# A mixture of experts computed on chosen tokens only, in sorted blocks of 128

## The reference

```
h = _ln(x, ln_g, ln_b)
logits = h @ rw.T + rb
vals, idx = jax.lax.top_k(logits, K)          # K = 2 of E = 8
gates = jax.nn.softmax(vals, axis=-1)
h1 = jax.nn.gelu(jnp.einsum('nd,efd->enf', hf, fc1_w) + fc1_b[:, None, :], approximate=False)
eo = jnp.einsum('enf,edf->end', h1, fc2_w) + fc2_b[:, None, :]
gathered = eo[idx_f, jnp.arange(N)[:, None], :]
mixed = (gathered * gates_f[..., None]).sum(axis=1).reshape(x.shape)
return x + mixed
```

## Time and profile before

| | |
|---|---|
| three runs | 3813.97, 3814.2, 3821.2 us; median 3814.2 |
| profiled execution | 3820.08 us; span from first to last instruction 3818.3 us |
| TensorE busy | 3622.8 us (95%), 32576 instructions |
| VectorE busy | 2628.9 us (69%) |
| ScalarE busy | 2835.2 us (74%) |
| GpSimd busy | 990.7 us (26%) |
| granted TensorE clock | 0.989 of full speed, mean |

### The profile page before, as it was taken

How to read it: one execution, slowest core, us unless ns; L and a number is a source line. 1 busy time by engine, 2 the same in 40 slices (tenths; PEclk the granted TensorE clock), 3 DMA queues, 4 the chain that set the end, 5 groups by cost and what they waited for, 6 DMA issues and landing times.

```text
span 3818.3 us, 86916 instructions
## 1 busy us (share of the span) xinstructions
PE 3622.8 (95%) x32576; PEld 2540.8 (67%) x32576; DVE 2628.9 (69%) x5516; ACT 2835.2 (74%) x4951; POOL 990.7 (26%) x1348
## 2 busy tenths in 40 slices
PE   6889999999999999999999999999999999999987
PEld 3556677676666767676676676766766676667764
DVE  7775666767676776767767667676767767666644
ACT  4677778777877778778787877778778777877645
POOL 2221222223132132322213222231322313222222
PEclk9999999999999999999999999999999999999988
DMA  2001001000010010000100010010100100000100
GB/s 66 2 3 47 34 14 32 25 24 23 12 43 14 24 33 24 21 14 24 34 24 21 14 32 25 24 34 6 39 14 24 34 23 21 14 26 25 37 12 7
DMA packets 52615, 92.56 MB, mean 24 GB/s; under 512 B 11816, under 2 KB 35312, under 8 KB 51952
## 3 DMA queue, kind: packets, MB, share of 16 engines
q1 hardware_dynamic: 52208, 87.01, 7.0%
HBM read 82.80 MB, written 4.19 MB: 23 GB/s over the span
## 4 chain that ended last, share of the span: by engine, by line
PE 73%; DVE 11%; ACT 7%; POOL 3%; issue 3%; DMA 1%; SPq 1%; DVEq 0%; ACTq 0%; POOLq 0%
PE ps L1277 14%; PE ps L1354 10%; PE ps L1346 9%; PE ps L1289 8%; PE ps L1267 7%; PE ps L1297 3%; PE ps L1236 3%; DVE mx L1649 3%; PE ps L1262 3%; PE ps L1309 2%; ACT pt L1502 2%; DVE pr L1655 2%; PE ps L1245 2%; PE ps L1314 1%; ACT xh L1452 1%
## 5 line engine op out<-in xcount | busy, mean ns | idle before, releaser
L1649 DVE TENSOR_REDUCE mx<-ps 128x8 f32<-128x616 f32 (+1 forms) x704 | 671.6, 954 | 352.3 <-PE ps L1267 335.4
L1502 ACT ACTIVATE pt<-ps 77x512 f32<-77x512 f32 (+1 forms) x1408 | 764.8, 593 | 126.3 <-PE ps L1277 124.3
L1277 PE MATMUL ps<-k_sb,pr 128*77 128x128 f32 (+1 forms) x3776 | 532.0, 280 | 13.5 <-DVE qT L1628 4.4
L1840 POOL TENSOR_TENSOR kx<-kT,in_tiles 128x308 f32<-128x308 f32 (+1 forms) x384 | 313.5, 817 | 808.9 <-PE ps L1267 741.1
L1493 ACT ACTIVATE pr<-pr 128x616 f32<-128x616 f32 (+1 forms) x472 | 393.3, 841 | 149.7 <-DVE pr L1655 149.0
L1346 PE MATMUL ps<-hT,ew 128*128 128x512 f32 x1024 | 488.0, 600 | 7.2 <-ACT kx L1541 2.3
L1277 PEld LDWEIGHTS ps<-k_sb,pr 128*77 128x77 f32 (+1 forms) x3776 | 416.5, 146 | 117.5 <-issue 71.2
L1655 DVE TENSOR_TENSOR pr<-ps,mx 128x616 f32<-128x616 f32 (+1 forms) x472 | 450.3, 954 | 16.2
L1289 PE MATMUL ps<-pt,v 77*16 77x128 f32 (+2 forms) x11264 | 428.5, 276 | 18.4 <-ACT pt L1502 16.2
L1289 PEld LDWEIGHTS ps<-pt,v 77*16 77x16 f32 (+2 forms) x11264 | 255.0, 97 | 218.0 <-issue 118.2
L1511 ACT ACTIVATE og<-ps 128x256 f32<-128x256 f32 x704 | 261.7, 378 | 184.6 <-PE ps L1289 181.7
(11 more groups left out here) (174 smaller groups left out, 6004.2 us busy)
## 6 DMA issues: line engine op xcount, KB each, us to landing
ew<-weights SPq DMA_DIRECT2D x128, 512.0 KB, 4.7
x<-x SPq DMA_DIRECT2D x16, 256.0 KB, 3.1
out<-xh SPq DMA_DIRECT2D x16, 256.0 KB, 2.5
...
w_sb<-weights SPq DMA_DIRECT2D x1, 1542.0 KB, 10.8
...
```

The costliest lines, as they stand in the source:

```text
L1277: i = tr(p[0:keys, j * L:(j + 1) * L], probs[s][pl.slot(unit, 3)][:, c:c + keys], ident)
L1502: go_act(pt[s][0:keys, q % 2, :], p[0:keys, :], ACT.Copy).then_inc(probsT_ready.sem, 1)
L1649: link(v_.tensor_reduce(m, tile, AX.X, ALU.max, negate=True))
L1840: tell(pool, g_.tensor_tensor(spread_keys[s][:, pl.slot(step, 2), 0:4 * keys].rearrange("p (h k) -> p h k", h=4), kT[s][:, b * keys:(b + 1 ...
```

## The change

The experts are computed only on the (token, expert) pairs that were chosen: 1024 pairs per pass, sorted by expert, each expert's pairs padded to blocks of 128. `BLOCKS` = 15 blocks always suffice. For each pass:

- `pick` (VectorE) ranks the logits and marks the two chosen experts. `place` (eight narrow matmuls on TensorE, some 22 short operations on VectorE) counts them and gives each pair its row in the sorted order, and each block its expert.
- `scatter`: GpSimd issues eight indirect DMAs that write the normalized rows `xh` to `sorted_x` in HBM, 128 rows of 512 bytes each. `sorted`: SyncE loads all 15 blocks back (983 KB) when they have landed. `sort_turn`: TensorE turns them, ScalarE applies gain and bias.
- `fetch`: GpSimd issues an indirect DMA per block that fetches one expert's packed row of 1156 floats per partition (fc1, fc2, and both biases) into one of four slots of `ew`, 15 per pass. Slot j is free after block j - 4.
- `up` is four matmuls of 128 columns per block, then one bias sum on VectorE over 128x512 and one gelu on ScalarE. `down` is four matmuls, then one sum on VectorE with the second bias.
- `put`: SyncE writes the results to `sorted_y` in HBM in four DMAs. `get`: GpSimd issues eight indirect DMAs that fetch each token's two rows. `combine`: eight scaled sums on VectorE.
- Once at the start, SyncE's queue copies the experts into a packed table `experts` in HBM (four DMAs after the load of pass 3), and fills `sorted_x` of each stream with finite numbers (983 KB each), that of stream 0 ahead of the first weights.
- `gates`, `expert_bias` and the resident second bias `b2_sb` are gone. The planner's costs of several other steps are changed by a few hundredths, and its priority tables (`EAGER`, `CHANGES`, `STRETCH` 60 to 80) are others, so the order on all engines is another.

```diff
+BLOCKS = 2 * NB * L // 128 + NE - 1
+GROUPS = -(-BLOCKS // 4)
+SLOTS = 4
...
-    out += [("fetch", s, 0), ("fetch", s, 1)]
-    out += norm_steps(6, s) + [("route", s), ("gates", s), ("expert_bias", s)]
-    for e in range(0, NE, 2):
-        out += [("up", s, f, c) for f in (e, e + 1) for c in range(FC)]
-        out += [("down", s, e), ("down", s, e + 1)]
-        if e + 4 < NE:
-            out.append(("fetch", s, e // 2 + 2))
+    out += norm_steps(6, s) + [("route", s), ("pick", s), ("place", s), ("scatter", s)]
+    out += [("fetch", s, j) for j in range(SLOTS)] + [("sorted", s)] + [("sort_turn", s, c) for c in range(GROUPS)]
+    for j in range(BLOCKS + 1):
+        if j < BLOCKS:
+            out.append(("up", s, j))
+        if j:
+            out.append(("down", s, j - 1))
+            if j + SLOTS - 1 < BLOCKS:
+                out.append(("fetch", s, j + SLOTS - 1))
+            if j % 4 == 0 or j == BLOCKS:
+                out.append(("put", s, (j - 1) // 4))
+    out += [("get", s), ("combine", s)]
...
     if kind == "fetch":
+        return [(G, INDIRECT), (Y, 3.4)]
+    if kind in ("scatter", "get"):
+        return [(G, 2 * NB * INDIRECT), (Y, 2.2)]
+    if kind == "sorted":
         return [(Y, 5.0)]
+    if kind == "put":
+        return [(Y, 3.0)]
...
+        "pick": [(V, 1.9)], "place": [(P, 0.9), (V, 5.0)], "combine": [(V, 2.5)],
+        "sort_turn": [(P, 0.47), (A, act(n, 1.2))],
+        "up": [(P, pe(128, 4) + 0.02), (V, 0.72), (A, act(n))], "down": [(P, pe(D, 4) + 0.04), (V, 0.3)],
...
-STRETCH = 60
+STRETCH = 80
...
+            sp.dma_start(sorted_x[0].rearrange("(p j) d -> p (j d)", p=128), weights[:, 0:BLOCKS * D]).then_inc(cleared[0], 16)
...
+                elif kind == "sorted":
+                    sp.wait_ge(scattered[s], 16 * 2 * NB * (s // S + 1))
+                    sp.dma_start(blocks[s], sorted_x[s].rearrange("(j p) d -> p j d", p=128)).then_inc(sorted_in[s], 16)
+                elif kind == "put":
+                    lo, hi = 4 * step[2], min(4 * step[2] + 4, BLOCKS)
+                    sp.wait_ge(*down_ready(s, hi - 1))
+                    sp.dma_start(sorted_y[s][lo * 128:hi * 128].rearrange("(j p) d -> p j d", p=128), blocks[s][:, lo:hi, :])\
+                        .then_inc(returned[s], 16)
...
+                    if s == S - 1:
+
+                        by_expert = experts.rearrange("(e p) n -> p e n", p=128)
+                        for name, source in (("fc1", weights[:, W_FC1:W_FC1 + NE * FF]), ("fc2", weights[:, W_FC2:W_FC2 + NE * FF]),
+                                             ("fc1_b", cols[:, C_AT["L1_fc1_b"][0]:C_AT["L1_fc1_b"][0] + NE * FC])):
+                            o, n = E_AT[name]
+                            sp.dma_start(by_expert[:, :, o:o + n], source.rearrange("p (e n) -> p e n", e=NE)).then_inc(packed, 16)
...
+                elif kind == "place":
+                    (s,) = args
+                    pe.wait_ge(*picked(s))
+                    flat = chosen[s][:].rearrange("p b e -> p (b e)")
+                    n = NB * NE
+                    mm(p[:, 0:n], K("upto"), flat, start=True, stop=False)
+                    for d in range(1, NB):
+                        mm(p[:, d * NE:n], ones[:], flat[:, 0:n - d * NE], start=False, stop=d == NB - 1)
                     for b in range(NB):
-                        i = tr(p[0:NE, b * L:(b + 1) * L], gates[s][:, b, :], ident)
-                    i.then_inc(gates_turned.sem, 1)
-                elif kind == "expert_bias":
-                    (s,) = args
-                    pe.wait_ge(*gT_ready(s))
-                    for b in range(NB):
-                        i = mm(p[:, b * D:(b + 1) * D], gT[s][:, b * L:(b + 1) * L], b2_sb[:], start=True, stop=True)
-                    i.then_inc(expert_bias_made.sem, 1)
+                        i = mm(p[:, n:n + NE], ones[:], chosen[s][:, b, :], start=b == 0, stop=b == NB - 1)
+                    i.then_inc(place_made.sem, 1)
+                elif kind == "sort_turn":
+                    s, c = args
+                    pe.wait_ge(sorted_in[s], 16 * (s // S + 1))
+                    for j in range(4 * c, min(4 * c + 4, BLOCKS)):
+                        i = tr(p[:, j % 4 * 128:(j % 4 + 1) * 128], blocks[s][:, j, :], ident)
+                    i.then_inc(sort_turned.sem, 1)
                 elif kind == "up":
-                    s, e, c = args
-                    if not c:
-                        pe.wait_ge(experts_fetched[e // 2 % 2], 32 * (2 * pl.holders[EXPERTS].index(s) + e // 4 + 1))
-                    mm(p[:, 0:NB * L], ew[:, e // 2 % 2, 0, e % 2 * FF + c * 128:e % 2 * FF + (c + 1) * 128], hT[s][:],
-                       start=True, stop=True)\
-                        .then_inc(up_made.sem, 1)
+                    s, j = args
+                    pe.wait_ge(*sort_ready(s, j // 4))
+                    before = pl.holders[EXPERTS].index(s) * len(range(j % SLOTS, BLOCKS, SLOTS))
+                    pe.wait_ge(experts_fetched[j % SLOTS], 16 * (before + j // SLOTS + 1))
+                    for c in range(FC):
+                        i = mm(p[:, c * 128:(c + 1) * 128], E(j % SLOTS, "fc1", c * 128, (c + 1) * 128),
+                               blocksT[s][:, j * 128:(j + 1) * 128], start=True, stop=True)
+                    i.then_inc(up_made.sem, 1)
                 elif kind == "down":
-                    s, e = args
-                    pe.wait_ge(*up_ready(s, e, FC - 1))
-                    for b in range(NB):
-                        for c in range(FC):
-                            i = mm(p[:, b * D:(b + 1) * D], h1[s][e % 2][:, c * NB * L + b * L:c * NB * L + (b + 1) * L],
-                                   ew[:, e // 2 % 2, 1, e % 2 * FF + c * D:e % 2 * FF + (c + 1) * D],
-                                   start=c == 0, stop=c == FC - 1)
+                    s, j = args
+                    pe.wait_ge(*up_ready(s, j))
+                    for c in range(FC):
+                        i = mm(p[:, 0:D], h1[s][j % 2][:, c * 128:(c + 1) * 128], E(j % SLOTS, "fc2", c * D, (c + 1) * D),
+                               start=c == 0, stop=c == FC - 1)
                     i.then_inc(down_made.sem, 1)
...
+                elif kind == "sort_turn":
+                    s, c = args
+                    lo, hi = 4 * c * 128, min(4 * c + 4, BLOCKS) * 128
+                    gain, bias = NORMS[6]
+                    act.wait_ge(*sort_turned(s, c))
+                    go_act(blocksT[s][:, lo:hi], p[:, 0:hi - lo], ACT.Identity, scale=C(gain), bias=C(bias))\
+                        .then_inc(sort_ready.sem, 1)
                 elif kind == "up":
-                    s, e, c = args
-                    act.wait_ge(*up_made(s, e, c))
-                    go_act(h1[s][e % 2][:, c * NB * L:(c + 1) * NB * L], p[:, 0:NB * L], ACT.Gelu, bias=C("L1_fc1_b", e * FC + c))\
-                        .then_inc(up_ready.sem, 1)
+                    s, j = args
+                    act.wait_ge(*up_biased(s, j))
+                    go_act(h1[s][j % 2], h1[s][j % 2], ACT.Gelu).then_inc(up_ready.sem, 1)
...
+                elif kind == "up":
+                    s, j = args
+                    dve.wait_ge(*up_made(s, j))
+                    if j >= 2:
+                        dve.wait_ge(*down_made(s, j - 2))
+                    tell(dve, v_.tensor_tensor(h1[s][j % 2].rearrange("p (c t) -> p c t", c=FC),
+                                               p.rearrange("p (c t) -> p c t", c=FC),
+                                               E(j % SLOTS, "fc1_b").unsqueeze(2).broadcast_to([128, FC, 128]), ALU.add),
+                         up_biased, s, j)
                 elif kind == "down":
-                    s, e = args
-                    dve.wait_ge(*down_made(s, e))
-                    for b in range(NB):
-                        i = v_.scalar_tensor_tensor(xs[s][:, b, :], p[:, b * D:(b + 1) * D], gates[s][:, b, e:e + 1],
-                                                    xs[s][:, b, :], ALU.mult, ALU.add)
-                    tell(dve, i, down_added, s, e)
+                    s, j = args
+                    dve.wait_ge(*down_made(s, j))
+                    tell(dve, v_.tensor_tensor(blocks[s][:, j, :], p[:, 0:D], E(j % SLOTS, "fc2_b"), ALU.add), down_ready, s, j)
...
+                elif kind == "combine":
+                    (s,) = args
+                    dve.wait_ge(answered[s], 16 * 2 * NB * (s // S + 1))
+                    for c in range(2):
+                        for b in range(NB):
+                            i = v_.scalar_tensor_tensor(xs[s][:, b, :], answers[s][:, c, b, :], found[s][:, c, 1, b:b + 1],
+                                                        xs[s][:, b, :], ALU.mult, ALU.add)
+                        if c == 0:
+                            link(i)
+                    tell(dve, i, combined, s)
...
+                elif kind == "scatter":
+                    (s,) = args
```

(28 more changed lines are left out.)

540 lines of the change are left out of this document (241 added, 299 removed).

## The result

Right after the prediction the changed kernel took 4005.35 us (median of four runs, 3992.49 to 4007.73) beside 3817.7 us for the kernel before (four runs, 3813.97 to 3830.5). The ratio is 1.0479 (95% interval 1.0462 to 1.0496): 4.8% slower. 3534 us and "faster" were forecast.

The account below looks back on a forecast made before the run. TensorE's work was taken to set the period: 3176 us of work plus 195.5 idle and 7 at the start gave 3379; with 54 for holds and 105 for in-order waits, span 3538, time 3534 us, range 3440 to 3640.

Parts of the forecast that it names:

- GpSimd's holds: Rival at scatter and get: the in-order queue stops three streams, whole 282 us appears, 3762 us; chance 0.20.
- The slower rival: Expert stage, exclusive to one pass: blocks served every 16 us, period 247 us, time 4068; chance 0.08.
- TensorE's sum: TensorE's work after removed and added matmuls and turns: 3176 us (3147 to 3232), 447 us less.
- The last paragraph of the prediction: Signs of error, among them a steady clock near 0.89 for more idle time: 357 us more.
- the holds: Scatter and get hold GpSimd's queue 8.8 us, delaying other streams' `spread`: 54 us taken, 0 to 282.
- in-order waits: VectorE and ScalarE queues, less free share, new order: steady idle of 6.6 us per period doubles, 105 us (0 to 211).
- 195.5 and 7: TensorE's idle time today, 195.5 us, plus 7 us start delay from the copy into `sorted_x[0]`.
- So I cost latency at nothing; its cover is that spread: Expert stage: even at twice the block time it takes 120 us, less than today's 165, so latency adds nothing.
- VectorE and GpSimd by load: Per pass of 205 us: VectorE 177 us, 86%; GpSimd 96 us, 47%, no bound by load.
- the gelu tables: ScalarE's gelu table loads, 113 now: lower end taken; loads near 240 would show the forecast wrong.

Follow-up runs that it names:

- e3: Changed kernel with scatter, get and the 15 weight fetches as plain DMAs from SyncE, fixed rows and experts, no indirect DMA: 3703.62 us.
- e19: The changed kernel, not edited, run again on a later occasion: 3776.46 us beside 3821.24 us for the kernel before, ratio 0.9892.
- last occasion: The later timing of the unedited changed kernel: 3776.46 us beside 3821.24 us for the kernel before, ratio 0.9892.
- first occasion: The timing of the changed kernel right after the prediction: 4005.35 us beside 3817.7 us for the kernel before, ratio 1.0479.
- e1: Changed kernel with scatter and get as plain DMAs from SyncE to and from fixed rows, the fetches still indirect on GpSimd: 3752.65 us.
- e6: As e1, with nine small GpSimd power operations standing where each scatter and get stood, no DMA issued from there: 3742.24 us.
- e12: Changed kernel with one small GpSimd power operation after every second issue of a scatter and get: 3921.18 us.
- e13: Changed kernel with one small GpSimd power operation after every issue of a scatter and get: 4048.59 us.
- e10: Kernel before with 32 times nine small GpSimd power operations added, no DMA: 3922.79 us (+103).
- e11: Kernel before with 256 indirect DMAs to scratch added, two at a time at eight places of a pass: 3875.72 us (+60).

## Why the prediction was wrong

The spans of four runs, as TensorE's busy and idle time:

| | busy | idle | span |
|---|---|---|---|
| forecast | 3176 | 362 | 3538 |
| e3, nothing by index | 3314.2 | 387.6 | 3701.8 |
| e19, last occasion | 3334.4 | 435.1 | 3769.5 |
| first occasion | 3432.5 | 573.4 | 4005.9 |

**The direction** failed at a step that isn't there: an issue by index was priced by what it takes of GpSimd's own time, and by what waits in its queue. Its effect on the other engines' signals, 4005.35 - 3776.46 = 229 us, was no term and no rival. Without it the change is 1.1% faster, so the direction would have been right and the time still 242 us over the forecast. The rival "GpSimd's holds" had the right place, scatter and get, and the wrong mechanism: TensorE waited only 7.2 us for `spread` before its scores (L1221), not 50. That e19's 3776 falls into the bracket of that rival (3640 to 3806) does not confirm it either: there the same wait is 9.3 us. The slower rival, a stage exclusive at 16 us a block, did not happen: from first fetch to last `down` a stage took 152 us on average on the first occasion, 10 us a block.

**TensorE's sum** was 158 us short even on the last occasion. Groups of e19, and behind them the one of before that answers to its first:

```profile
L1243 PE MATMUL ps<-pt,v 77*16 77x128 f32 (+2 forms) x11264 | 453.0, 279 | 49.3 <-ACT pt L1461 30.2 <-DVE pr L1622 8.9 <-DVE kx L1712 4.0
L1221 PE MATMUL ps<-kx,qT 32*128 32x308 f32 (+2 forms) x2816 | 362.6, 548 | 54.6 <-ACT pt L1461 19.9 <-POOL kx L1880 9.3 <-DVE pr L1622 8.9
...
L1307 PE MATMUL ps<-pr,ew 128*128 128x128 f32 x1920 | 261.6, 280 | 24.6 <-DMA ew<-experts,expert_row 12.8 <-DVE x L1646 3.5 <-DVE kx L1622 3.1
L1314 PE MATMUL ps<-ew,pt 128*128 128x128 f32 x1920 | 260.3, 279 | 7.5 <-ACT pt L1503 4.9 <-DVE pr L1622 1.0 <-DVE xh L1632 0.7
```
```profile
L1289 PE MATMUL ps<-pt,v 77*16 77x128 f32 (+2 forms) x11264 | 428.5, 276 | 18.4 <-ACT pt L1502 16.2 <-DVE pr L1655 1.6 <-ACT kx L1541 0.3
```

The expert matmuls are 521.9 us, 0.272 each, inside the range of 0.235 to 0.279 but 42 us over the 0.25 taken; `place` and the turns of the sorted blocks together took 74 us, 70 forecast. Most of the rest lies in work that the change doesn't touch: the mixing matmuls (L1243 now, L1289 before) took 428.5 us and take 453.0, the scores 355.1 and 362.6. Added up over all groups that both kernels have, it is 3002.8 us before, 3082.6 in e3, 3100.1 in e19 and 3193.1 on the first occasion, so 97 of the 158 us in e19. (Groups overlap, so these sums are above TensorE's busy time; a smaller overlap accounts for some 14 us more.) The mean granted clock over the run is 0.989 before, 0.966 in e19 and 0.934 on the first occasion. As a mean of the levels 2.4 and 1.2 GHz, that is some 84, 256 and 529 us at the lower one. The last paragraph of the prediction named this: more idle time, a lower clock. As an estimate, 3176 us at 0.966 in place of 0.989 is 76 us more, at 0.934 187 us more. So two terms were mis-sized: every kept matmul was priced at the clock of a kernel that is 97% busy in its steady stretch, and a new one at 0.25 us, though a matmul in steps of four already took 0.279. What makes up the remaining part of the kept work's 97 us, beside the clock, was not taken apart.

**Idle time.** 54 for the holds and 105 for in-order waits were added to 195.5 and 7. e3 has no holds at all and yet 387.6 us, 192 over the kernel before; near the upper end of that term (0 to 211), not at its 105. Between e3 and e19 idle time grows by 48 us. That it is near the 54 of the holds is luck: 25 of the 48 are there in e1 already (412.9 us idle), which has only the fetches by index, and e6 says that standing as planned costs nothing by itself. Outputs in SyncE's queue of e19 (start, us, what), then windows of e19 and of the kernel before, each up to the first output, from it to the twelfth, and from there on:

```profile
700.69 0.38 SPq L1144 DMA_DIRECT2D out<-xh  x1
...
3102.89 0.38 SPq L1144 DMA_DIRECT2D out<-xh  x1
...
3608.54 153.27 SPq L1144 DMA_DIRECT2D out<-xh  x3
```
```profile
0.00:700.70 700.70, 604.45 (x5852) 425.97 (x5853) 524.26 (x1039) 487.35 (x876) 242.29 (x318) 0.98 0.21 64
700.70:3102.90 2402.20, 2179.79 (x20963) 1590.70 (x20962) 1846.46 (x3829) 1782.17 (x3135) 975.38 (x1213) 0.98 0.19 59
3102.90:3769.50 666.60, 550.16 (x4791) 396.72 (x4789) 427.61 (x959) 409.13 (x717) 260.74 (x313) 0.92 0.19 58
```
```profile
0.00:661.10 661.10, 589.81 (x5353) 402.74 (x5354) 452.10 (x897) 462.70 (x819) 154.32 (x221) 0.99 0.08 27
661.10:3200.90 2539.80, 2470.02 (x22405) 1739.27 (x22404) 1800.29 (x3785) 1967.88 (x3423) 681.32 (x925) 1.00 0.08 24
3200.90:3818.30 617.40, 563.01 (x4823) 398.82 (x4821) 376.55 (x835) 404.64 (x711) 155.04 (x203) 0.96 0.07 22
```

In the middle the forecast nearly held. Eleven periods from the first output take 218.4 us each; they took 230.9 in the kernel before (first output 661.14, twelfth 3200.92), and 214 was forecast. TensorE is idle 222 us there, 20.2 a period, where it was idle 70, or 6.3 a period. The forecast had 6.6 doubled, and 3.4 for a hold: 16.6. So most of the new idle time (153 of 240 us) lies in the middle, and most of it was in the sum.

What failed is the ends. The middle is 138 us shorter than before. But the first output comes 39.6 us later, and from the twelfth to the last it takes 658.5 us, not 614.6: 84 us lost. The forecast scaled the whole span by TensorE's sum, ends and all, and so had the ends shrink. Of the 231 us between its span of 3538 us and e19's 3769.5, the middle has 11 x 4.4 = 48 and the ends have 183. The sentence that failed is "So I cost latency at nothing; its cover is that spread". It holds while four streams run. At both ends fewer do, and routing, scatter, load, blocks and get stand in a row. From the twelfth output on TensorE is idle 116 of 667 us at a clock of 0.92, where before it was idle 54 of 617 at 0.96. The rows show the loss at the ends; that it is this latency is argued. e3, which has no issue by index at all, loses 58 of the 84 us as well (outputs from 692.88, the twelfth at 3057.77, the last at 3699.1), so most of it belongs to the stage and to the new order, which no run tells apart.

**Right:** VectorE and GpSimd by load, no bound; the gelu tables; 5.5 us for a fetch (5.4 forecast, where the estimate from the Trainium skill, DMA: Bandwidth & Descriptors, section on the anatomy of a GpSimd-issued DMA, gave 3.4); an issue at 1.0 us in 0.39 to 2.24; `up` hardly waiting for weights. By the Trainium skill, SBUF — State Buffer, section on its two separate sides, descriptor writing by GpSimd waits out VectorE's two-port operations. No run here shows it: an issue took 0.95 to 1.0 us on average on both occasions, 1.37 us at the longest, beside a VectorE busy for 70 or 74% of the span.

**What an unplanned hold costs.** e12 has 142.7 us more of GpSimd's busy time than e19, and takes 144.7 us longer; e13 284.4, and 272.1 (they ran in different sets, whose kernels before are 6 us apart). Here is e12's page (busy, chain), and TensorE's waits for `spread`:

```profile
PE 3392.1 (87%) x31600; PEld 2452.7 (63%) x31600; DVE 2802.1 (71%) x5826; ACT 2680.7 (68%) x4726; POOL 1621.1 (41%) x1973
...
PE 45%; DVE 20%; POOL 12%; ACT 11%; issue 7%; DMA 3%; SPq 1%; POOLq 0%; DVEq 0%; ACTq 0%
```
```profile
PE ps L1217 <- POOL kx L1886: 46.9, 10, 8.0
PE ps L1222 <- POOL kx L1886: 27.9, 5, 14.0
```

GpSimd has 12% of its chain, 6% in e19. The two waits, 74.8 us together, are 22.5 in e19 and 128.2 in e13: this is the mechanism that the rival "holds" described, and it comes with holds that the plan doesn't have. So here GpSimd, busy 39% of the span, passed such a hold on one for one. It is no rule: in the kernel before, e10's 291 us of unplanned standing cost 103 us, and e11's 256 issues in pairs, 264 us of GpSimd's busy time, cost 60.
